# Channel mix in pieces between the attention heads, q/k/v projections in a stage ahead of them, and low halves of the streamed weights on POOL

## The reference

```
x + time/channel mix(xn) + attention/MoE(xn)

time mix:     x2  = xn + sigmoid(mix @ Wr) * (vmix @ Wo + bo)
channel mix:  xc  = ln(ln(x2));  xcs = xc shifted by one token
              kc  = square(relu(xcs @ Wck))        # 512 -> 2048
              out1 = x2 + sigmoid(xc @ Wcr) * (kc @ Wcv)   # 2048 -> 512
attention:    q, k, v = rmsnorm(xn) @ Wq.T, Wk.T, Wv.T     # 16 heads of 32, causal softmax
              xp  = xn + heads @ Wo.T
MoE:          8 experts, the best two per token, silu(x @ Wg) * (x @ Wu) @ Wd, weighted
              out2 = xp + moe(rmsnorm(xp))
```

## Time and profile before

| | us |
|---|---|
| median of 3 runs | 2159.82 |
| the profiled execution, its own time | 2163.49 |
| its span, first to last instruction | 2161.7 |
| PE busy | 1914.1 (89%) |
| DVE, ACT, POOL busy | 1202.4, 935.3, 551.5 |
| mean granted clock of PE | 0.922 of full |

### The profile page before, as it was taken

One profiled execution on the slowest core, in us unless ns is written; L12 is line 12 of the kernel. 1 busy time (PEld: TensorE's weight loads), 2 busy tenths in 40 slices (PEclk: granted clock), 3 DMA queues, 4 the chain that ended last, 5 costly groups with the idle time before them and its releaser, 6 DMA issues. The chain is left out here.

```text
span 2161.7 us, 30419 instructions
## 1 busy us (share of the span) xinstructions
PE 1914.1 (89%) x10850; PEld 1634.4 (76%) x10850; DVE 1202.4 (56%) x1794; ACT 935.3 (43%) x1505; POOL 551.5 (26%) x536
## 2 busy tenths in 40 slices
PE   3878667898889889767999997999999999999997
PEld 2666455686677676555888886999999999999986
DVE  6887334835726736543555557555555555555543
ACT  4454333634625525422222222555555555555553
POOL 3233220010010010152000004334444353434443
PEclk9989876996996987877999998999999999999998
DMA  4332352251270260270002015756666565756562
GB/s 175 118 117 97 137 156 60 79 144 33 78 168 8 78 157 1 78 277 9 32 19 79 0 40 208 280 196 202 201 213 216 203 209 201 228 196 206 193 194 49
DMA packets 70275, 288.21 MB, mean 133 GB/s; under 512 B 10375, under 2 KB 10631, under 8 KB 51922
## 3 DMA queue, kind: packets, MB, share of 16 engines
q1 hardware_dynamic: 56514, 262.84, 35.0%
q0 software_dynamic: 11552, 20.55, 5.6%
q10 hardware_dynamic: 2160, 4.19, 0.5%
HBM read 220.47 MB, written 45.84 MB: 123 GB/s over the span
## 5 line engine op out<-in xcount | busy, mean ns | idle before, releaser
L49 PE MATMUL bank<-ex_x_hi,ex_w_hi 128*128 128x256 f32 x1472 | 419.0, 285 | 5.2 <-issue 5.2
L50 PE MATMUL bank<-ex_x_lo,ex_w_hi 128*128 128x256 f32 x1472 | 417.4, 284 | 0.0
L51 PE MATMUL bank<-ex_x_hi,ex_w_lo 128*128 128x256 f32 x1472 | 417.3, 284 | 0.0
L1215 DVE TENSOR_TENSOR ex_w_lo<-ex_stage,ex_w_hi 128x2048 fp32r<-128x2048 f32 x138 | 249.9, 1838 | 147.4 <-ACT ex_w_hi L1160 141.0
L49 PEld LDWEIGHTS bank<-ex_x_hi,ex_w_hi 128*128 128x128 f32 x1472 | 283.1, 192 | 8.2 <-issue 5.6
L50 PEld LDWEIGHTS bank<-ex_x_lo,ex_w_hi 128*128 128x128 f32 x1472 | 283.2, 192 | 2.7
L51 PEld LDWEIGHTS bank<-ex_x_hi,ex_w_lo 128*128 128x128 f32 x1472 | 283.1, 192 | 0.0
L1099 POOL TENSOR_TENSOR ex_a_lo<-ex_a,ex_a_hi 128x256 fp32r<-128x256 f32 x184 | 176.6, 980 | 393.5 <-ACT ex_a_hi L1180 381.5
L1175 ACT ACTIVATE ex_gate<-bank 128x256 f32<-128x256 f32 x184 | 70.7, 384 | 240.7 <-PE bank L51 240.7
L721 ACT ACTIVATE cm_relu<-bank 128x512 f32<-128x512 f32 x64 | 38.3, 599 | 256.8 <-PE bank L51 220.7
L1943 PE MATMUL bank<-at_k,at_q 96*128 96x512 f32 (+3 forms) x256 | 115.4, 546 | 38.0 <-DMA at_k<-at_ones 26.9
(11 more groups left out here) (268 smaller groups left out, 4484.1 us busy)
## 6 DMA issues: line engine op xcount, KB each, us to landing
ex_stage<-in_w_moe SPq DMA_DIRECT2D x69, 1536.0 KB, 6.3
first_w<-in_w_moe SPq DMA_DIRECT2D x23, 1536.0 KB, 7.5
at_q<-at_q_hi SPq DMA_DIRECT2D x32, 256.0 KB, 5.2
at_k<-at_k_hi SPq DMA_DIRECT2D x32, 256.0 KB, 6.3
cm_stage<-in_w_cm SPq DMA_DIRECT2D x8, 1024.0 KB
tm_x_in<-in_x SPq DMA_DIRECT2D x4, 1024.0 KB, 7.2
scratch_xn<-tm_xn SPq DMA_DIRECT2D x4, 1024.0 KB, 5.3
tm_xn_res<-scratch_xn SPq DMA_DIRECT2D x4, 1024.0 KB, 9.0
```

Source lines behind the costliest of these rows:

```text
L49: pe.matmul(out, lhsT=w_hi, rhs=x_hi, start=first, stop=False)
L50: pe.matmul(out, lhsT=w_hi, rhs=x_lo, start=False, stop=False)
L51: return pe.matmul(out, lhsT=w_lo, rhs=x_hi, start=False, stop=last)
L1215: return dve.tensor_tensor(dst, src, hi.bitcast(F32), ALU.subtract)
```

## The change

The attention and channel mix blocks go. In their place stand `project_phase` and `heads_phase`.

`project_phase` computes q, k (as halves) and v for all four sequences in a row, without heads between, and writes them to DRAM (five 1 MB DMAs per sequence, each ahead of the next sequence's).

`heads_phase` runs the 64 heads of all sequences as one pipeline of 71 steps (lag 5 in place of 8). q, k and v come back from DRAM, per head six DMAs of 32 partitions into one of 8 slots (`load_slot`). Between the heads stand **pieces**: 144 in all, each 12 matmuls of 512 columns on one bank. An `up` piece is 128 hidden features of one sequence, a `down` piece sums 4 of them (512 hidden features) for 128 tokens, a `proj` piece is the attention's output projection for 128 tokens. Channel mix is now done sequence after sequence, in blocks of 4 ups and 4 downs, so each weight slice (128x512) is loaded and split once per sequence, four times in all: 144 slices with those of `proj`. ACT makes the high half of a slice, POOL the low half. The first 10 pieces come two per step, then 94 in the 59 steps that follow (one or two per step), then two per step, and the last 26, the projection of the last sequence and most of its channel mix, come after the heads. There is one bank for ups and one for sums, two for scores, two for turned scores, one for the output of heads. ACT makes `p_hi` of all heads. The result is no longer summed in SBUF: SP copies `x` to `out`, and POOL adds `x2`, `xp` and the channel mix onto it by accumulating DMAs, each of which waits for the one before. The router's chain and its 32 indirect DMAs stand among the last 26 pieces; the first expert's weights are loaded after them. In `experts_phase` only the write of `acc` and the wait for it go. Time mix frees its semaphores at its end, with one more barrier.

```diff
+def heads_phase(nc, psum, ident, ident_bf, causal, causal_t, routing, first_tile, route, d):
+    N = B * HEADS
+    LAG = 5
+    SLOTS = 8
+    SET = 4
+    RAW = 6
+    DEEP = 4
+    CHUNKS = I_CM // (DEEP * P)
+    STEPS = N + LAG + 2
...
+    def pieces_before(s):
+        early = 2 * min(s, LAG)
+        middle = 94 * min(max(s - LAG, 0), N - LAG) // (N - LAG)
+        late = 2 * max(s - N, 0)
+        return early + middle + late
...
+        def _(sp):
...
+            load_slot(0)
+            for w in range(RAW):
+                load_slice(w)
+            load_slot(1)
+            load_mix(0)
+            for g in range(2, SLOTS):
+                load_slot(g)
+            sp.dma_start(vecs[:, :, :], d["vecs"]).then_inc(const_in, 16)
+            sp.dma_start(wr[:, :, :], d["w_r"]).then_inc(const_in, 16)
...
+            for b in range(B):
+                sp.dma_start(d["out"][b * S:(b + 1) * S, :].rearrange("(p r) h -> p (r h)", p=P),
+                             d["x"][b].rearrange("(p r) h -> p (r h)", p=P)).then_inc(x_out, 16)
...
+        def _(pool):
...
+            def weight(w):
+                kind, b, c, m = slices[w]
+                pool.wait_ge(w_hi_ready, w + 1)
...
+                pool.tensor_tensor(lo, raw[:, w % RAW, :], hi.bitcast(F32), ALU.subtract).then_inc(w_lo_ready, 1)
+            for w in range(DEEP):
+                weight(w)
+            pool.wait_ge(x_out, 16 * B)
+            for b in range(B):
+                pool.dma_start(d["out"][b * S:(b + 1) * S, :].rearrange("(p r) h -> p (r h)", p=P),
+                               d["x2"][b].rearrange("(p r) h -> p r h", p=P), accum_op=ALU.add, max_dma_last_dim=4 * H).then_inc(added, 16)
+            def add_rows(k, b, j, src):
+                pool.wait_ge(added, 16 * adds_before[k])
+                at = b * S + j * P
+                pool.dma_start(d["out"][at:at + P, :], src[:, j, :], accum_op=ALU.add, max_dma_last_dim=4 * H).then_inc(added, 16)
+            for k in range(PIECES):
+                for w in fresh[k]:
+                    weight(w)
...
+                if k == count_at + 2:
+                    pool.wait_ge(table_filled, 16)
+                    pool.wait_ge(route.step, route.SLOTS)
...                            # 32 indirect DMAs
+        def _(act):
...
+            for s in range(STEPS):
+                i = s - LAG
+                ks = pieces(s)
+                for k in late:
+                    finish(k)
+                for k in ks[:1]:
+                    begin(k)
+                if 0 <= i < N:
+                    exps(i, 0)
+                    exps(i, 1)
+                for k in ks[:1]:
+                    finish(k)
+                if 1 <= i <= N and i % 2 == 0:
+                    inverse_sums(i // 2 - 1)
+                if 0 <= i < N:
+                    exps(i, 2)
+                    high_p(i)
+                if s % 2 == 0 and 0 <= s // 2 - 2 < N // 2:
+                    high_v(s // 2 - 2)
+                if s % 2 == 0 and 0 <= s // 2 - 4 < N // 2 and (s // 2 - 4) % PAIRS >= HC:
+                    high_o(s // 2 - 4)
+                for k in ks[1:]:
+                    begin(k)
+                if s % SET == 0 and SET <= s <= N:
+                    max_row(s // SET - 1)
+                late = ks[1:]
...
+        def _(pe):
...
+            pe.wait_ge(x_zero, 3)
+            pe.wait_ge(consts_ready, CONSTS)
+            pe.wait_ge(const_in, 32)
+            for s in range(STEPS):
+                i = s - LAG
+                ks = pieces(s)
+                if s < N:
+                    scores(s, 0)
+                    scores(s, 1)
+                for k in ks[:1]:
+                    piece(k)
+                if s < N:
+                    scores(s, 2)
+                if 0 <= i < N:
+                    turned(i, 0)
+                    turned(i, 1)
+                if 1 <= i <= N:
+                    head_output(i - 1)
+                if 0 <= i < N:
+                    turned(i, 2)
+                for k in ks[1:]:
+                    piece(k)
+                if s % SET == 0 and SET <= s <= N:
+                    turn_maxima(s // SET - 1, misc_free[0])
```

## The result

The changed kernel takes 2202.33 us (median of 4 runs, 2198.56 to 2204.80) against 2159.29 us for the kernel before: ratio 1.0197, interval [1.0176, 1.0217]. Forecast were 2175 and slower. The sign and the shape were right, the size was not: +43 us where +15 was said.

A forecast was written before the change was run, and what follows sets the result against it. PE's own sequence was taken as the bound. Time mix to 268, projections to 445, start to 515, middle to 1183, tail and barrier to 1350, plus 826 of experts gave 2176, put on the median 2175 us; range 2095 to 2245.

The forecast's parts named there:

- project phase, with the barrier before it: From time mix's end: 1 us for the barrier, then 176 us for q, k, v of four sequences and the end.
- start, to the fifth piece: Start of the heads block: waits for `const_in`, then for low halves behind POOL's additions; 70 us, ends 50 and 100.
- middle, to the end of piece 117: Interleaved steps from the fifth piece to the last step: 595 us of PE work plus 73 us of stalls, 668 us.
- tail, gap and barrier, to the experts' first: Last 26 pieces with their stalls to the end, 164 us with ends 130 and 190, then the barrier.
- largest term: In the tail, PE stands still for 36 us, waiting for POOL's low halves queued behind 32 indirect DMAs.
- 16 x 1: Middle: row maxima at every fourth step pass PE, DVE and ACT before scores are accepted; put at 17 us.
- 0.3 of handing over: Middle: 0.3 us for handing over, counted in the up-to-up stalls and again in the up-to-down stalls.
- 595 + 73 = 668: Middle: 595 us of PE alone (heads, pieces, transposes, logits) plus 73 us of stalls make 668 us.
- The clock I take as 1.00: Middle: PE's clock would be 1.00, since it was 0.98 to 1.00 where dense matmuls had preceded.
- Rival 1: Faster: ACT frees banks within two scores, stalls 25 rather than 73 us, start 50 rather than 70; 2110 us, chance 0.37.
- Rival 2: Slower: POOL's subtractions under the heads hold up DVE's `p_lo`, costing 50 us; 2225 us, chance 0.13.
- Rival 3: Slower: stalls between pieces leave PE at 1.2 GHz in a fifth of 600 us, +120; 2295 us, chance 0.06.

The follow-up runs named there:

- spreading the DMAs: Against the changed kernel, the router's 32 indirect DMAs no longer stand in a row: three follow each piece's low halves from piece 129 on; 2177.1 us.
- alternating banks: Against the changed kernel, sums in the last 26 pieces alternate between two banks, and so do ups after piece 127; 2188.0 us.
- control: The changed kernel itself, unaltered, run again as base of the later runs; 2201.5 us, ratio 1.0279 to the kernel before.
- short halves: Against the changed kernel, POOL's 136 later subtractions cover only 16 of 512 columns, leaving low halves of the weights incomplete; 2182.6 us.
- list of pieces: Against the changed kernel, only how many pieces stand in each of the 71 steps is changed, 118 in all as before; 2203.1 us.
- list and short halves: Against the changed kernel, new counts of pieces per step together with POOL's later subtractions cut to 16 of 512 columns; 2166.3 us.

## Why the prediction missed by 27 us

By its own steps, on the profiled run (its span, 2196.8, against 2176):

| step | forecast | measured | difference |
|---|---|---|---|
| project phase, with the barrier before it | 177 | 166.0 | -11 |
| start, to the fifth piece | 70 | 60.6 | -9 |
| middle, to the end of piece 117 (1201.5) | 668 | 706.9 | +39 |
| tail, gap and barrier, to the experts' first | 167 | 167.1 | 0 |
| experts | 826 | 828.2 | +2 |

Project phase and start: `const_in` took 30.75 for 32, and the first down waited 9.1 us behind the additions of `x2` and, ahead of them, the copies into `out`; both sums were on the careful side. The clock of the projections was 0.92, not the 1.00 that I had named. Tail: right in sum and in its largest term (36 forecast, 32.7 measured, and shown by spreading the DMAs). Two slips in the working change little: 16 x 1 is 16, not 17, and the 0.3 of handing over has no row; in the trace PE starts 0.10 to 0.15 us after the instruction of DVE that it waited for. What I had lumped as single small stalls are per-piece costs of 1.15 and 1.78 us, and the alternating banks took 12 to 20 us of them away.

**The step that failed is the middle**, "595 + 73 = 668", and in it "The clock I take as 1.00". The idle time itself came out as forecast: 71.3 us (80.4 less 9.1) for 73, in part by luck, for the shares are others (the first downs and ups 38 for 38, `head_output` 18 for 14, the maxima 4 for 17, and 6.5 for low halves of POOL that I hadn't priced). The next profile was to show these waits ended mostly by ACT; DVE and POOL end them. Two things were taken as nothing in the sum, and they make 34 of the 39 us:
- Starting again after a wait cost 0.27 us beyond the idle time, as read between the pieces of the tail. Some 68 waits make 18 us, an estimate.
- The clock was 0.97. Summed over the matmuls inside pieces that start 0.43 us apart instead of 0.23, that is 16 us. It didn't fall as in the first part of heads before (0.71), but its mean was not 1.00 in any run (0.92 to 0.99).

The reason that the prediction gave for 1.00, dense matmuls ahead, was misread from the earlier trace rows: ahead of the heads' stretch at 0.98 stood the heads' stretch at 0.71, and the stretch right behind the dense projections, with PE busy for 11 of 20 us, had 0.58:

```profile
328.00:348.00 20.00, 11.05 (x45) 7.79 (x45) 8.09 (x21) 3.17 (x10) 0.00 (x0) 0.58 0.53 121
```

595 + 71 + 18 + 16 = 700 of 706.9; the heads' own matmuls at the lower clock aren't in the 16. The restarts go with the number of waits, and POOL's subtractions raise that number (72 in the control, 58 with short halves). The clock doesn't go with it: 0.96 with 58 waits, 0.99 with 72. It rose where the list of pieces was combined with another change, 0.98 with short halves and 0.99 with low halves on DVE. What it is in the list that does this stays open. With the list and short halves the middle is 34 us under the control: 25 less standing and 9 less busy.

**The rivals.** Rival 1 (side engines keep up, stalls of 25 us) failed: PE stood still for 51.0 us or more of the middle in every run. Rival 2 had the right mechanism with a third of its price. Its sign, `p_lo` over 1.8 us at the mean, is met (1.847), and its cost is 17 us by short halves, 31 at the most, with what POOL's own slowness adds, not 50. I set it beside the forecast as an alternative, at 0.13; it should have been a term in the sum, since the earlier trace rows had shown it for equal tiles. Rival 3 (clock of 1.2 GHz in a fifth of the stretch) had a seventh of its 120 us.

The remaining 6 to 7 us between 21 on the profile and 27 on the medians are run scatter: the profiled run of before was 3.7 us above its median, that of the changed kernel 3.8 us below.

Not tested: a second bank in the middle, and `p_hi` taken from ACT again. So the 51 us of standing that are left without POOL's subtractions aren't put down to the single banks by any run.

As for the change as a whole: in the first measurement it lost 35 us over the two blocks in profiles. Projections ahead of the heads gained some 14 us: before, they took 20.1 us to the first and then four stretches of 39.1 to 40.6 us, together 180, now 166.0. Interleaving exchanged two dense blocks for waits at single banks, and the two pieces of code that stood behind POOL's queue (low halves behind 32 DMAs, and beside DVE) cost 33 us in the tail and 17 to 31 in the middle. With the low halves on DVE, another order at the start, two banks in the tail and the new list of pieces, the same design takes 2128.7 us.

## What to carry to other kernels

Work moved to an idle engine must be looked at in that engine's queue, not in its busy share: POOL was 34% busy and still cost the most, once by 32 DMAs in front of an urgent subtraction, once by holding up DVE. When a profile shows an operation stretched by a neighbour, put that into the sum as a term, with the longest and the mean of its row as bounds. And count waits as well as their idle time: each restart of PE had a price of its own. Put the clock into the sum as a term with bounds, too: it was 0.92 to 0.99 in this stretch, whatever the number of waits. When two changes to an order are tried one by one, each can show nothing while both together gain.

## What the runs showed of the hardware that I had not expected

- PE needed some 0.27 us beyond the idle time when it started again between pieces (4.53 - 2.75 - 1.50, and 3.89 - 2.75 - 0.88).
- The interference of DVE and POOL goes both ways: `p_lo` 1493 to 1847 ns at the mean, POOL's subtraction 1252 to 1564 and 1612.
- An accumulating DMA of 1 MB cost POOL no more than about 1.1 us (four in 4.46), while 32 tiny indirect ones cost 1.27 us each from issue to issue.
- The time of the kernel before was 18 us lower in all later runs, on four chips, than in the first measurement, and that of the changed kernel lower by less than 1. No run here says why.
